# Attention units of two heads by 512 queries instead of four heads by 256, with VectorE inverting the softmax sums straight from PSUM

## The reference

```
x = x + linear_attention(group_norm(x))          # L0: q, k normed per head, dots = k^T v, out = q dots / n
t = x + softmax_attention(layer_norm(x))         # L1:
      q, k, v = z @ w_qkv^T, split in 8 heads
      attn = softmax(q k^T / sqrt(32)); out = (attn v) @ w_agg^T + b_agg
t = t + experts(layer_norm(t))                   # FFN: sinkhorn gates (8 rounds of column and row scaling),
                                                 # each of 8 experts takes its top 128 tokens of an image
```

## Time and profile before

| | |
|---|---|
| median of 3 runs | 1469.5 us (1467.96 to 1470.09) |
| span of the profiled execution | 1467.7 us; no total of its own is recorded, so the medians' 1.8 us above it are taken as what lies around a span |
| PE / DVE / ACT / POOL busy | 1339.3 / 1021.3 / 868.7 / 562.6 us |
| score matmuls, line 894 | 2048 of 96x256, 342.1 us busy |
| `add_up`, line 1635 | 512 + 128 of 128x512, 331.3 + 98.4 us |
| inversion, line 1609 | 64 of 128x256, 111.4 us |
| granted TensorE clock | 0.950 of full speed over the span |

### The profile page before, as it was taken

How to read it: one execution, slowest core, us unless ns; L and a number is a source line. 1 busy time by engine, 2 the same in 40 slices (tenths; PEclk the granted TensorE clock), 3 DMA queues, 4 the chain that set the end, 5 groups by cost and what they waited for, 6 DMA issues and landing times.

```text
span 1467.7 us, 29142 instructions
## 1 busy us (share of the span) xinstructions
PE 1339.3 (91%) x10849; PEld 915.8 (62%) x10849; DVE 1021.3 (70%) x2114; ACT 868.7 (59%) x1268; POOL 562.6 (38%) x1068
## 2 busy tenths in 40 slices
PE   5789989999999999999999999999998999987535
PEld 3556656667576767676767676656666567766423
DVE  3536766858585857586768676787789776899771
ACT  2456557677667767677666767665675667542100
POOL 1132530445134513551245214520554116875443
PEclk9899989999999999999999999999999999999665
DMA  2051013600360037002710272005500265454322
GB/s 79 29 137 51 1 30 87 172 16 27 80 184 15 2 93 193 18 2 75 184 46 2 57 168 79 2 30 117 144 15 2 65 169 191 128 158 134 118 68 80
DMA packets 66785, 119.13 MB, mean 81 GB/s; under 512 B 10705, under 2 KB 46546, under 8 KB 66642
## 3 DMA queue, kind: packets, MB, share of 16 engines
q1 hardware_dynamic: 57682, 90.48, 22.9%
q0 software_dynamic: 8960, 26.75, 6.0%
HBM read 29.11 MB, written 33.55 MB: 43 GB/s over the span
## 4 chain that ended last, share of the span: by engine, by line
PE 62%; DVE 24%; issue 6%; POOL 4%; ACT 3%; DMA 0%; DVEq 0%; POOLq 0%; ACTq 0%
PE shared L938 30%; PE scores L894 12%; PE acc L916 11%; DVE prob_sum L1635 6%; PE acc L913 3%; PE shared L933 3%; DVE acc_sb L1609 2%; DVE bn L1344 2%; ACT probs L1209 2%; DVE work L1543 1%; PE acc L926 1%; DVE resid L1350 1%; DVE best_i L1541 1%; DVE best L1539 1%; DVE bn_x L1404 1%
## 5 line engine op out<-in xcount | busy, mean ns | idle before, releaser
L1209 ACT ACTIVATE probs<-scores 128x1024 f32<-128x1024 f32 x512 | 516.0, 1024 | 178.1 <-PE scores L894 94.0
L894 PE MATMUL scores<-query_stack,key_stack 96*128 96x256 f32 x2048 | 342.1, 308 | 16.0 <-ACT probs L1209 15.7
L1635 DVE TENSOR_TENSOR prob_sum<-prob_sum,probs 128x512 f32<-128x512 f32 x512 | 331.3, 707 | 0.0
L894 PEld LDWEIGHTS scores<-query_stack,key_stack 96*128 96x128 f32 x2048 | 275.9, 192 | 85.1 <-issue 39.1
L916 PE MATMUL acc<-probs,v_all 128*32 128x256 f32 x4096 | 289.2, 389 | 0.0
L1242 POOL TENSOR_TENSOR attn_T<-acc_sb 128x256 f32<-128x256 f32 x56 | 41.4, 740 | 447.8 <-DVE acc_sb L1609 445.0
L938 PE MATMUL shared<-w_sb,chan 128*128 128x512 f32 (+1 forms) x512 | 186.7, 501 | 5.9 <-DVE chan L1438 5.9
L916 PEld LDWEIGHTS acc<-probs,v_all 128*32 128x32 f32 x4096 | 114.8, 110 | 104.0 <-issue 37.9
L938 PEld LDWEIGHTS shared<-w_sb,chan 128*128 128x128 f32 x512 | 91.9, 192 | 62.5 <-issue 57.9
L938 PE MATMUL shared<-chan,w1T 128*128 128x512 f32 x256 | 121.3, 608 | 2.1 <-ACT chan L1125 2.1
L1635 DVE TENSOR_TENSOR prob_sum<-probs 128x512 f32<-128x512 f32 x128 | 98.4, 810 | 18.8 <-ACT probs L1209 16.5
(11 more groups left out here) (220 smaller groups left out, 2036.7 us busy)
## 6 DMA issues: line engine op xcount, KB each, us to landing
query_stack<-hi SPq DMA_DIRECT2D x120, 128.0 KB, 2.5
key_stack<-hi SPq DMA_DIRECT2D x120, 128.0 KB, 2.5
x_sb<-in_x_dram SPq DMA_DIRECT2D x8, 1024.0 KB, 5.3
out_dram<-resid SPq DMA_DIRECT2D x16, 512.0 KB, 4.8
tokens_scratch<-resid SPq DMA_DIRECT2D x16, 512.0 KB, 5.5
tokens_scratch<-rows SPq DMA_DIRECT2D x16, 512.0 KB, 3.3
key_stack<-lo SPq DMA_DIRECT2D x60, 128.0 KB, 2.5
query_stack<-lo SPq DMA_DIRECT2D x60, 128.0 KB, 2.5
```

The costliest lines, as they stand in the source:

```text
L894: last = pe.matmul(score_ps[u % 2][:, QB * r:QB * (r + 1)], key_stack[stack, HG * g + r, P * kt:P * (kt + 1)], query_stack[stack, HG * g + ...
L1209: act.activation(probs[:, u % PROBS, :], score_ps[u % 2][:, :], ACT.Exp, scale=DH ** -0.5) \
L1635: dve.tensor_tensor(total[:, part], probs[:, (u - 1) % PROBS, part] if kt == 1 else total[:, part], probs[:, u % PROBS, part], ALU.add).th ...
```

## The change

A unit is now 2 heads x 128 keys x 512 queries. A slot still has two units (now the two pairs of heads for the same 128 keys), a block has 8 slots and 512 queries, an image has 4 blocks. Exponentials stay as many and as wide; score matmuls are half as many and twice as wide.

- `prob_sum` has one part for each pair of heads. The exponential of kt 0 is written straight into it, and `add_up` for kt 1 to 5 adds one `probs` buffer in one instruction of 1024 columns. In a block of 8 slots DVE adds in slots 1 to 5.
- `acc` holds only the product with v. The sums go to one of the three shared banks, which is held from slot 6 of a block until slot 0 of the next is over; meanwhile the other steps have two banks.
- `total` runs in slot 6, not at the end of the block.
- ACT copies `acc` without the sums (128x512, but half as often). DVE inverts the sums from PSUM in two instructions of 256 columns, one after the other, in the middle of slot 0 of the next block. POOL multiplies in two halves.
- The last blocks' queries come later, so the table moves `agg` 4 to 7 back and `x_stats`, `gmean` forward.
- The scratch of the software DMA queue is halved to 8192 bytes a partition.

```diff
-QB = 256
+QB = 512
 NQB = N // QB
-BLOCK_UNITS = T
-UNITS = G * NQB * BLOCK_UNITS
-PAIRS = UNITS // 2
-BLOCK_PAIRS = BLOCK_UNITS // 2
+HALF = QB // 2
+UNIT_HEADS = HG // 2
+UNIT = UNIT_HEADS * QB
+BLOCK_SLOTS = T
+BLOCKS = G * NQB
+SLOTS = BLOCKS * BLOCK_SLOTS
...
-             ("store_stats", 0), ("xT", 1, 1), ("xT", 0, 0), ("agg", 4), ("agg", 5), ("x_stats",), ("agg", 6),
-             ("store_rows", 0), ("rest", 1), ("agg", 7), ("gmean",), ("store_rows", 1), ("store_rows", 2),
-             ("gvar",), ("store_stats", 1), ("z2T", 0), ("store_rows", 3), ("z2T", 1), ("z2T", 2), ("z2T", 3),
+             ("store_stats", 0), ("xT", 1, 1), ("xT", 0, 0), ("x_stats",), ("store_rows", 0), ("gmean",),
+             ("store_rows", 1), ("rest", 0.5), ("agg", 4), ("agg", 5), ("agg", 6), ("gvar",), ("agg", 7),
+             ("store_rows", 2), ("store_stats", 1), ("z2T", 0), ("store_rows", 3), ("z2T", 1), ("z2T", 2), ("z2T", 3),
...
+def bank_uses(plan, freed_scores):
+    uses, times, turn, held = {}, [0] * (SHARED + 4), 0, None
+    def take(s, banks):
+        nonlocal turn
+        while turn % banks == held:
+            turn += 1
+        i = turn % banks
+        uses[s] = i, times[i]
+        times[i] += 1
+        turn += 1
+        return i
+    for n, slot in enumerate(plan):
+        banks = SHARED + 4 if n >= freed_scores else SHARED
+        kt = None if slot.pair is None else slot.pair % BLOCK_SLOTS
+        for second, half in enumerate(slot.halves):
+            for s in half:
+                if s[1][0] not in BANKLESS:
+                    take(s, banks)
+            if kt == T - DIRECT and not second:
+                held = take((None, ("total", slot.pair // BLOCK_SLOTS)), banks)
+        if kt == 0 or slot.pair is None:
+            held = None
     return uses
...
-    probs = sb("probs", [P, PROBS, HG * QB])
-    prob_sum = sb("prob_sum", [P, HG * QB])
-    acc_sb = sb("acc_sb", [P, BANK])
+    probs = sb("probs", [P, PROBS, UNIT])
+    prob_sum = sb("prob_sum", [P, 2, UNIT])
+    acc_sb = sb("acc_sb", [P, 2, QB])
...
-                for r in range(HG):
-                    last = pe.matmul(score_ps[u % 2][:, QB * r:QB * (r + 1)],
-                                     key_stack[stack, HG * g + r, P * kt:P * (kt + 1)],
-                                     query_stack[stack, HG * g + r, QB * qb:QB * (qb + 1)], start=True, stop=True)
+                for r in range(UNIT_HEADS):
+                    h = HG * g + UNIT_HEADS * pair + r
+                    last = pe.matmul(score_ps[pair][:, QB * r:QB * (r + 1)], key_stack[stack, h, P * kt:P * (kt + 1)],
+                                     query_stack[stack, h, QB * qb:QB * (qb + 1)], start=True, stop=True)
...
+                pe.wait_ge(s["exp_done"], 2 * k + 2)
+                if kt > added:
+                    ps, i, nth = bank(None, ("total", blk))
+                    if kt == added + 1 and nth:
+                        pe.wait_ge(s[f"read{i}"], nth)
+                    for r in range(HG):
+                        last = pe.matmul(ps[DH * r:DH * (r + 1), :], ones[:, 0:DH], head_probs(k, r),
+                                         start=kt == added + 1, stop=kt == T - 1, skip_group_check=True,
+                                         tile_position=(0, DH * r))
+                    if kt == T - 1:
+                        last.then_inc(s[f"full{i}"], 1)
...
+                ps, _, _ = bank(None, ("total", blk))
                 pe.wait_ge(s["summed"], 2 * added * (blk + 1))
                 for r in range(HG):
-                    last = pe.matmul(acc_ps[DH * r:DH * (r + 1), QB:2 * QB], ones[:, 0:DH],
-                                     prob_sum[:, QB * r:QB * (r + 1)], start=False, stop=True,
-                                     skip_group_check=True, tile_position=(0, DH * r))
-                last.then_inc(s["blocks_done"], 1)
+                    last = pe.matmul(ps[DH * r:DH * (r + 1), :], ones[:, 0:DH],
+                                     prob_sum[:, r // UNIT_HEADS, QB * (r % UNIT_HEADS):QB * (r % UNIT_HEADS + 1)],
+                                     start=False, stop=False, skip_group_check=True, tile_position=(0, DH * r))
+                last.then_inc(s["totalled"], 1)
...
-                    weigh(2 * k)
-                    weigh(2 * k + 1)
-                    if k % BLOCK_PAIRS == BLOCK_PAIRS - 1:
-                        total(k // BLOCK_PAIRS)
+                    weigh(k)
+                    if k % T == added + 1:
+                        total(k // T)
...
-                act.wait_ge(s["blocks_done"], blk + 1)
-                await_count(act, "attn_ready", blk)
-                act.activation(acc_sb[:, :], acc_ps[:, :], ACT.Copy) \
-                   .then_inc(s["acc_copied"], 1)
+                act.wait_ge(s["weighed"], T * (blk + 1))
+                await_count(act, "attn_ready", 2 * blk)
+                act.activation(acc_sb[:, 0, :], acc_ps[:, :], ACT.Copy).then_inc(s["acc_copied"], 1)
...
+                if k % T == 0:
+                    await_count(act, "totalled", k // T)
+                else:
+                    n = before_in_buffer(k)
+                    if n >= 0:
+                        act.wait_ge(s["weighed"], n + 1)
+                    if n >= 0 and n % T <= added:
+                        act.wait_ge(s["summed"], 2 * (added * (n // T) + n % T - 1) + pair + 1)
+                act.activation(unit_probs(k, pair), score_ps[pair][:, :], ACT.Exp, scale=DH ** -0.5) \
                    .then_inc(s["exp_done"], 1)
...
+                pool.wait_ge(s["acc_copied"], blk + 1)
...
+                for h in range(2):
+                    part, tokens = slice(HALF * h, HALF * (h + 1)), QB * qb + HALF * h
+                    pool.wait_ge(s["recip_ready"], 2 * blk + h + 1)
+                    pool.tensor_tensor(attn_T[:, g, tokens:tokens + HALF], acc_sb[:, 0, part], acc_sb[:, 1, part],
+                                       ALU.mult).then_inc(s["attn_ready"], 1)
...
-                dve.wait_ge(s["acc_copied"], blk + 1)
-                dve.reciprocal(acc_sb[:, QB:2 * QB], acc_sb[:, QB:2 * QB]).then_inc(s["recip_ready"], 1)
+                ps = await_full(dve, None, "total", blk)
+                await_count(dve, "attn_ready", 2 * blk)
+                for h in range(2):
+                    part = slice(HALF * h, HALF * (h + 1))
+                    dve.reciprocal(acc_sb[:, 1, part], ps[:, part]).then_inc(s["recip_ready"], 1)
+                dve.wait_ge(s["recip_ready"], 2 * blk + 2)
+                dve.sem_inc(s[f"read{bank(None, ('total', blk))[1]}"], 1)
...
+            def add_up(k, pair):
+                kt, total = k % T, prob_sum[:, pair, :]
+                dve.wait_ge(s["exp_done"], 2 * k + pair + 1)
+                if kt == 1:
+                    dve.wait_ge(s["weighed"], k)
+                else:
+                    dve.wait_ge(s["summed"], 2 * (added * (k // T) + kt - 2) + pair + 1)
+                dve.tensor_tensor(total, total, unit_probs(k, pair), ALU.add).then_inc(s["summed"], 1)
...
-                if k is not None:
-                    if k % BLOCK_PAIRS < BLOCK_PAIRS - 1:
-                        add_up(2 * k)
-                    add_up(2 * k + 1)
+                if k is not None and 1 <= k % T <= added:
+                    add_up(k, 0)
+                    add_up(k, 1)
+                elif k and k % T == 0:
+                    invert(k // T - 1)
                 for st in second:
                     step(*st)
-                if k and k % BLOCK_PAIRS == 0:
-                    invert(k // BLOCK_PAIRS - 1)
...
-    nc = _bacc.Bacc("TRN2", target_bir_lowering=False, num_devices=1)
+    nc = _bacc.Bacc("TRN2", target_bir_lowering=False, num_devices=1, dynamic_dma_scratch_size=8192)
     arrays, args = {}, []
     for name in _INS:
         a = _np.ascontiguousarray(inputs[name])
```

136 lines of the change are left out of this document (56 added, 80 removed).

## The result

The changed kernel takes 1567.03 us (median of 4, 1565.58 to 1568.52), the kernel before 1469.26 on the same chip (4 runs). The ratio is 1.067, with an interval of 1.0656 to 1.0686. Forecast was 1502 in a range of 1450 to 1520: the direction was right, the size not. The slowdown is 98 us instead of 33.

A forecast was written before the change was run, and what follows sets the result against it. PE was taken to bound the middle of the program. 1467.7 - 23 (wider scores) + 50 (waits in six segments) + 6 (the rest) = 1500.7 us, plus 1.8 around it: 1502.5, stated as 1502, range 1450 to 1520.

The forecast's parts named there:

- PE's gain: Score matmuls: four of 512 columns replace eight of 256, 0.09 us less a slot, 23 us over 256 slots.
- This rival: Score matmuls: width gives nothing, a wide one takes 0.24 us; 1525 us in all, chance 0.06.
- The wait for the mean: Slot 1 of a segment: PE wants `gmean` at 9.3 us, the mean is ready at 14.2; 4.9 us.
- Scores of slot 7: Second pair's scores wait for the second kt 6 exponential, held up by late additions; 1.8 us a segment.
- `lin` behind `dots`: Slot 17: the first `lin` directly follows `dots` and waits for two VectorE instructions; 0.8 us a segment.
- Slots 19 to 21: VectorE's additions, `lin` and statistics take 12.2 us against PE's 9.6; 1.2 us left on PE a segment.
- Slot 8: `v0` 0 needs the bank of `qk0` 2, which ACT must have copied; 0.3 us a segment.
- The clock: Rival: the six segments, PE at 94%, are granted 0.98, adding 15 us: 1517 us; chance 0.20.
- Inversion from PSUM: VectorE's inversions of 256 columns keep the same 1.65 us spacing from PSUM; 0 to 10 us in all.
- Additions: VectorE's additions of 1024 columns take 1226 ns, 1.145 us each in sequence, 2.29 us a slot; 18 us off VectorE.
- The last segment with attention: POOL's and ACT's reads of `turn` and `expert` on two banks in three places; 2 us (-2 to 8).
- The tail: Behind the last block, two inversions precede the first quotient, `agg` 4 to 7 follow; 2.5 us (0 to 8).

The follow-up runs named there:

- the fillers: Four overwritten fp32 matmuls of 512 columns ahead of `gmean`: in the changed kernel 1553.6 us, in the kernel before with `gmean` early and the old rest 1505.3 us.
- the filler: The changed kernel with four fp32 matmuls of 512 columns, overwritten by `gmean`, ahead of it in the attention segments: 1553.6 us.
- at_kt3: The changed kernel with the old table, sums copied by ACT, and kt 3's two additions cut to 64 of 1024 columns: 1494.6 us.
- a_rows: The changed kernel with `store_rows` 0 put behind `agg` 4 and `store_rows` 1 behind `agg` 7 in the table: 1564.0 us.
- b_rest: The kernel before, with the rest of one slot in its step table cut to half a slot: 1535.4 us.
- a_rest: The changed kernel with a rest of one slot, not half, ahead of `agg` 4 in its table: 1539.8 us.

## Why the prediction was wrong, step by step

The direction and the place were right: VectorE's answers behind PE's questions, from the table. By its own steps:

- **PE's gain** (-23 us): failed. It was 0 to 4. The 0.215 came from fp32 matmuls, and by halving once too often: the four records of 1.72 us are the passes of two matmuls, as the fillers show (four matmuls, eight records, 3.70 us). So a pass of 512 columns in fp32 takes 0.43, and no row had 0.215 for one in fp32r. A wide score matmul takes 0.236 where two narrow ones take 0.240. The page "VectorE: DVE Perf Modes" of the Trainium skill (section on the TRN2 errata), with 6 cycles and the columns, had the consequence right, no gain, by 0.87 us for either form. Both are in fact 9 to 10% longer than by that rule (0.120 and 0.236 for 0.109 and 0.216). This rival, priced at 0.24 each and given 0.06, is what the chip does.
- **The wait for the mean** (4.9): right in place and cause, 3.64 in size. With the 1.06 for `agg` 2, which the forecast had inside it, 4.7.
- **Scores of slot 7** 1.8: measured 1.40 + 0.40. **`lin` behind `dots`** 0.8: 1.21. **Slots 19 to 21** 1.2: 0.80 + 0.40. **Slot 8** 0.3: 0.34 + 0.26 on ACT's copies. The timeline was good to a few tenths, in one place by luck: of 12.2 us against 9.6 with a slot of lag free, some 0.6 should be left in slots 19 to 21, not 1.2. In all 10.6 us of idle a middle segment, for 9.0.
- **The clock** (0 in the forecast, a rival of 0.20 with 15 us): mis-sized. By the granted clock of 0.98 the middle segment shown lost 3.3 to 3.4 us, the second to fifth segments between 1.6 and 5, and the filler took back 11 us in all. The rival reasoned from PE's mean load; the rows put the fall behind single waits. Which waits bring it stays open: the two segments of at_kt3 have the same waits and the same work. (And 2% of the rival's 900 us is 18, not 15.)
- A middle segment is PE's busy 153.07, of which 3.4 come from the clock, and 10.6 idle: 163.7. The forecast had 149.3 - 2.9 + 9.0 = 155.4. So of the 8.3 us missing per segment, 3.3 are PE's own rate (149.7 of work for 146.4), 3.4 the clock (an estimate, from half of 6.8 us), 1.6 the waits.
- **Inversion from PSUM** at the same price: right (1719 ns). **Additions**: a median of 1217 ns for 1226, so the slope held; the mean is 1257, as about one in ten takes 1.3 to 2.1 us. Two on end take 2.34 us, for 2.29. Both small.
- **The last segment with attention** (2 less 2.9): failed, +13.7. With the old table it is still +7.1 (159.2). ACT queues its exponentials behind `store_rows`, for which POOL's root isn't ready: 6.45 us at once. That the table now has these rows ahead of `agg` 4 explains 1.7 of them (a_rows). I had looked there for waits on banks.
- **The tail** 2.5 (0 to 8): 6.8. PE waits 5.46 for the first quotient, for 1.12; both inversions run ahead of it.
- **Which part costs what** was half wrong. The forecast put the waits of `lin` and of slots 4 to 8 down to units and bank. The kernel before has the one of `lin` too once half a slot of rest is gone (b_rest), and the changed kernel loses all of them when it is given back (a_rest): it is the shift of all later steps, which I read in the table and did not price.

What stays open: of the 42 us that the units cost with the old table, the tail has 6.6, the last segment 7. In a middle segment 1.1 is for `agg` 2 (0.76 with ACT's copy, gone without inversions), 1.5 in slots 19 to 21 (gone without kt 3), 1.16 for ACT behind POOL (gone with narrow additions); the 1.1 for `gvar` stayed in all three. That it shows because PE's long `weigh` with the sums and `total` stood in slot 3 before, and a short one stands there now, is argued from the order and was not tried.

## What to carry to other kernels

When an order is tuned so tightly that the busiest engine has no idle time, a shift of every step by half a slot can cost more than the edit that it comes with: price the moves of the table first, each by itself, then the new instructions. A rate must come from the same kind of instruction. And a wider instruction on one engine can hold another engine's short ones for its whole length, as VectorE's additions held POOL's here; look for short instructions whose duration grew.
